# Attention with feed-forward on 8 cores: heads and output tiles transposed by DMA, and side work planned by its length

## The reference

```python
r = layernorm(x)                      # x: 4 x 4096 x 1024
q = einsum('bnd,hkd->bnhk', r, Wq)    # 16 heads of 64
k = einsum('bmd,dk->bmk', r, Wk)      # one key head, shared by all
v = einsum('bmd,dv->bmv', r, Wv)
o = softmax(q k^T / 8) v
x = x + einsum('bnhv,dhv->bnd', o, Wp)
s = layernorm(x) @ Win + bin          # 64 values per token
g = sum_h relu(s[..., None] * W1 + b1) * W2 + b2   # 16 inner values each
x = x + g @ Wout + bout
```

## Time and profile before

| | |
|---|---|
| time, median of 3 runs | 1017.74 us (1017.22 to 1017.86) |
| time of the profiled execution | 1017.6 us |
| its span on the slowest core | 1016.1 us (the 8 cores: 1012.9 to 1016.1) |
| busy: PE, PEld, DVE, ACT, POOL | 900.6, 493.1, 358.7, 952.2, 56.5 us |
| granted TensorE clock, mean of a core | 0.986 to 0.989 |
| chain that ended last | ACT 80%, issue 9%, PE 5%, DVE 3%, DMA 3% |

### The profile page before, as it was taken

One profiled execution on the slowest core, in us unless ns is written; L12 is line 12 of the kernel. 1 busy time (PEld: TensorE's weight loads), 2 busy tenths in 40 slices (PEclk: granted clock), 3 DMA queues, 4 the chain that ended last, 5 costly groups with the idle time before them and its releaser, 6 DMA issues.

```text
span 1016.1 us, 28595 instructions; the slowest of 8 cores (1012.9 to 1016.1 us)
## 1 busy us (share of the span) xinstructions
PE 900.6 (89%) x11582; PEld 493.1 (49%) x11712; DVE 358.7 (35%) x637; ACT 952.2 (94%) x1043; POOL 56.5 (6%) x131
## 2 busy tenths in 40 slices
PE   3898899998899999998889999998889998898884
PEld 3445555555444545544444454544444554454442
DVE  4535666652512222234202122244202326424215
ACT  2597999999999999999999999999999999999981
POOL 3201111100000000000000000000000000000000
PEclk9999999999999999999999999999999999999995
DMA  8502257220000000002200000001210000400101
GB/s 196 138 12 85 85 119 174 85 85 3 1 2 2 2 2 2 2 2 84 85 2 2 1 3 1 2 2 62 58 51 2 2 2 2 167 2 1 44 2 41
DMA packets 13406, 40.94 MB, mean 40 GB/s; under 512 B 3168, under 2 KB 3296, under 8 KB 13152
## 3 DMA queue, kind: packets, MB, share of 16 engines
q1 hardware_dynamic: 8208, 26.26, 8.5%
q0 software_dynamic: 4784, 12.32, 5.3%
q10 hardware_dynamic: 288, 0.52, 0.1%
HBM read 35.70 MB, written 8.39 MB: 43 GB/s over the span
## 4 chain that ended last, share of the span: by engine, by line
ACT 80%; issue 9%; PE 5%; DVE 3%; DMA 3%; POOL 0%; DVEq 0%; SPq 0%; POOLq 0%; ACTq 0%
ACT ptu L816 80%; DMA xtra<-x_own 2%; PE ob L457 1%; DMA xbuf<-x_own 1%; PE spa L662 1%; PE spb L662 1%; DVE r1u L478 1%; PE sda L380 0%; DVE r1t L504 0%; DVE lnst L468 0%; PE spb L695 0%; DVE lnst L469 0%; DVE gacc L787 0%; POOL rstd L838 0%; PE sdb L391 0%
## 5 line engine op out<-in xcount | busy, mean ns | idle before, releaser
L816 ACT ACTIVATE ptu<-spa 128x1024 bf16<-128x1024 f32 x512 | 594.5, 1161 | 17.7 <-PE spa L662 17.6
L816 ACT ACTIVATE ptu<-spb 128x1024 bf16<-128x1024 f32 x512 | 595.9, 1164 | 2.9 <-PE spb L662 2.9
L457 PE MATMUL ob<-vab,ptu 128*128 128x65 bf16 x8192 | 409.1, 195 | 0.7 <-ACT ptu L816 0.5
L457 PEld LDWEIGHTS ob<-vab,ptu 128*128 128x128 bf16 x8192 | 298.4, 97 | 208.4 <-issue 208.4
L662 PE MATMUL spb<-qt,k2t 64*128 64x512 bf16 x1024 | 200.8, 380 | 40.5 <-ACT ptu L816 34.9
L662 PE MATMUL spa<-qt,k2t 64*128 64x512 bf16 x1024 | 200.9, 380 | 36.5 <-ACT ptu L816 28.3
L662 PEld LDWEIGHTS spb<-qt,k2t 64*128 64x128 bf16 x1024 | 63.4, 92 | 127.2 <-issue 108.1
L662 PEld LDWEIGHTS spa<-qt,k2t 64*128 64x128 bf16 x1024 | 62.6, 92 | 114.5 <-issue 95.1
L725 DVE TENSOR_TENSOR oacc<-oacc,ob 128x520 f32<-128x520 f32 x50 | 34.8, 696 | 77.3 <-PE ob L457 77.2
L836 POOL TENSOR_SCALAR lnve<-lnmv 128x1 f32<-128x1 f32 x48 | 12.7, 264 | 658.0 <-DVE lnmv L471 658.0
L527 DVE TENSOR_TENSOR xbuf<-xbuf,sda 128x512 f32<-128x512 f32 x16 | 11.0, 688 | 93.3 <-PE sda L423 80.0
(11 more groups left out here) (123 smaller groups left out, 471.1 us busy)
## 6 DMA issues: line engine op xcount, KB each, us to landing
xbuf<-x_own SPq DMA_DIRECT2D x28, 512.0 KB, 4.4
xbuf<-x_oth SPq DMA_DIRECT2D x16, 512.0 KB, 3.9
out<-xbuf POOLq DMA_DIRECT2D x14, 512.0 KB, 3.6
wqb<-wq POOLq DMA_DIRECT2D x8, 256.0 KB, 9.6
xtra<-x_own SPq DMA_DIRECT2D x4, 512.0 KB, 6.9
xtra<-wp POOLq DMA_DIRECT2D x1, 2048.0 KB, 21.0
boutbc_s<-boutbc SPq DMA_DIRECT2D x1, 512.0 KB, 12.7
out<-xbuf SPq DMA_DIRECT2D x2, 256.0 KB, 2.6
```

Source lines behind the costliest of these rows:

```text
L457: r = te.matmul(osum[:, hd, c * 65:(c + 1) * 65], ptu[:, g % NPT, hd * 512 + c * 128:hd * 512 + (c + 1) * 128], vab[:, a + i, :], start=(i ...
L816: sc.activation(ptu[:, g % NPT, :], sps[g % 2][:], AF.Exp, scale=0.125).then_inc(ex, 1)
```

## The change

- The 31 "ot" transposes (all but the last pair of heads) and the 14 "rt" transposes leave PE and DVE. SP issues DMA transposes instead, from `on` to `ot` and from r1u to r2t, in an order (`moves`) that `pace` writes down; "op" and "s2" wait for their semaphores. In block 3 a pair of heads takes two DMAs.
- The loads of x for output tiles 4 to 15 move from SP to POOL, behind the stores of the tiles before them; wp is loaded in 8 DMAs instead of one.
- `pace` weighs pieces: a slot is 92 (hundredths of a us), scores 22, a half 12, a PE piece 22; a piece goes in while PE is at most 25 behind. DVE pieces have lengths of their own, and a tile's statistics are two pieces.
- What the value product needs is forced behind the scores, no longer ahead of them; V of slab 0 comes ahead of the first scores. K of slab 1 is made in two parts, three tiles and one. All queries of block 1 come at the end of block 0's list, those of block k + 1 in block k.
- r1u holds 4 tiles instead of 2.

```diff
-    o = [("V", 0, 0)] + q(0, 1) + slab(1) + [("V", 1, 0)]
-    o += q(0, 2, 3, 4, 5, 6, 7)
+    o = [("V", 0, 0)] + q(0, 1) + slab(1) + [("V", 1, 0)] + q(0, 2, 3, 4, 5, 6, 7)
     for s in range(2, NSLAB):
         o += slab(s) + [("V", s, 0)]
-    return o + q(1, 0) + [("ot", 0, hp) for hp in range(NHP - 1)]
+    return o + q(1, *range(NHP))
 def output_parts(b):
...
 def output_parts(b):
     op = [[("op", 4 * b + t, h) for h in range(2)] for t in range(4)]
-    rt = [("rt", 4 * b + t, 0) for t in range(4)]
     fo = [("fo", 4 * b + t, h) for t in range(4) for h in range(2)]
-    return [op[0], op[1], rt[0:1] + op[2], rt[1:2] + op[3], rt[2:4], [("s2", b, 0)], fo[0:4], fo[4:8]]
+    return op + [[], [("s2", b, 0)], fo[0:4], fo[4:8]]
...
-    queries = [("Q", 1, c) for c in range(1, NHP)] + [("Q", k, c) for k in (2, 3) for c in range(NHP)]
     o = []
     for p in range(24):
         k, i = 1 + p // NHP, p % NHP
         if i == 0:
-            o += [("ot", k - 1, NHP - 1)]
             parts = output_parts(k - 1)
-        for _ in range(1 + p % 2):
-            o += [queries.pop(0)] if queries else []
-        o += [("ot", k, i - 1)] if i else []
+        o += [("Q", k + 1, i)] if k < LAST else []
         if k < LAST:
             o += parts[i]
         elif i < 4:
             o += parts[2 * i] + parts[2 * i + 1]
         else:
             o += [[("op", 12, 0), ("op", 12, 1), ("op", 13, 0), ("op", 13, 1)],
...
+SLOT = 92
+SCORES = 22
+SWITCH = 20
+HALF = 12
+PIECE = 22
+PE_LAG = 25
+TR_LAG = 6
...
+    def force(want, where):
+        n = 0
+        while not ok(want, -TR_LAG):
+            mm = [("smd", v) for name, v in want if name == "sev"]
+            if not ok(mm, 0) and ok(head["pe"], -TR_LAG):
+                run("pe", pe, "pe" + where)
+                n += 1
+            else:
+                assert head["dve"] is not None and ok(head["dve"][0], -TR_LAG), (now, head)
+                run("dve", dve, "dve" + where)
+        return n
...
+            if g == -2:
+                want.append(("sev", USE_NO["V", 0, 0] + 1))
+            forced += force(want, "_s")
...
-        while not ok(want, 0):
-            if head["pe"] is not None and ok(head["pe"], 0):
-                run("pe", pe, "pe0")
-            else:
-                assert head["dve"] is not None and ok(head["dve"], 0), (g, head)
-                run("dve", dve, "dve0")
+                note("otd", 8 * SEGS[s][0] + SEGS[s][1] + 1, TR_LAG)
+            dve_lag += 110 if last_part(s) else 75
...
-        halves = len(pv_at(s, g - SEG_AT[s]))
-        for _ in range({0: 2, 2: 1, 3: 0}[halves]):
-            if head["pe"] is not None and ok(head["pe"], 1):
-                run("pe", pe, "pe1")
-
-        if g + 1 != SEG_AT[s + 1] and head["dve"] is not None and ok(head["dve"], 1):
-            run("dve", dve, "dve1")
-    return counts
+        halves = pv_at(s, g - SEG_AT[s])
+        forced += force([("sev", USE_NO["V", (SEGS[s][2] + h // 2) // 4, 0] + 1) for h in halves], "_v")
+        pe_lag = min(pe_lag + PIECE * forced, PE_LAG)
+        t = SCORES + HALF * len(halves) + (SWITCH if halves or forced else 0)
+        switch = 0 if halves or forced else SWITCH
+        while head["pe"] is not None and ok(head["pe"], 1):
+            if pe_lag + t + switch + PIECE - SLOT > PE_LAG:
+                break
+            run("pe", pe, "pe")
+            t += switch + PIECE
+            switch = 0
+        pe_lag = max(0, pe_lag + t - SLOT)
+        room = SLOT + (20 if g + 1 in SEG_AT else 115)
+        while head["dve"] is not None and ok(head["dve"][0], 1) and dve_lag + head["dve"][1] <= room:
+            dve_lag += head["dve"][1]
+            run("dve", dve, "dve")
+        dve_lag = max(0, dve_lag - SLOT)
+    return counts, moves
...
                 elif kind == "K":
-                    yield [("sev", n)]
-                    wait_ev(te, n - 1)
-                    for j in range(DCH):
-                        if j:
-                            yield []
-                        r = te.matmul(bank[:], wkb[:, j, :], r1t[:, slab_buf(a), j, :],
-                                      start=(j == 0), stop=(j == DCH - 1))
+                    parts = [(0, 3), (3, 4)] if a == 1 else [(0, 4)]
+                    for t0, t1 in parts:
+                        tr = USE_NO["tr", 4 * a + t1 - 1, 0]
+                        cols = slice(128 * t0, 128 * t1)
+                        for j in range(DCH):
+                            if j == 0:
+                                yield [free, ("sev", tr + 1)]
+                                wait_ev(te, n - 2)
+                                wait_ev(te, tr)
+                            elif j % (4 if t1 - t0 == 1 else 1) == 0:
+                                yield []
+                            r = te.matmul(bank[:, cols], wkb[:, j, :], r1t[:, slab_buf(a), j, cols],
+                                          start=(j == 0), stop=(j == DCH - 1))
...
-                    done = USE_NO["ot", blk, {0: NHP - 1, 12: 3, 14: 6}[a // 2 * 2 if blk == LAST else 0]]
-                    yield [free, ("sev", done + 1)]
+                    done = 8 * blk + ({12: 3, 14: 6}[a // 2 * 2] if blk == LAST else NHP - 1)
+                    yield [free, ("otd", done + 1)]
                     if a == 0 and b == 0:
-                        te.wait_ge(wpl, 16)
+                        te.wait_ge(wpl, 16 * DCH)
                     wait_ev(te, n - 2)
-                    wait_ev(te, done)
+                    te.wait_ge(otl[done % 2], heads_moved(done))
+                    te.wait_ge(otl[1 - done % 2], heads_moved(done - 1))
...
-                    yield [("sev", n)]
+                    li = NTILES + GROUPS[a][-1]
+                    yield [free, ("trd", li + 1)]
                     if a == 0:
                         te.wait_ge(winl, 16)
-                    wait_ev(te, n - 1)
+                    wait_ev(te, n - 2)
+                    for t in GROUPS[a]:
+                        te.wait_ge(trl[t % 4], 16 * (t // 4 + 1))
...
+            elif li < NTILES + 4:
+                if li >= 8:
+                    v.wait_ge(smd, USE_NO["tr", li - 4, 0] + 1)
+            else:
+                v.wait_ge(trl[q], 16 * ((li - NTILES) // 4))
+            v.tensor_scalar(r1u[:, q, :], xt(li), lnmv[:, q, 0:1], rstd[:, q, :],
                             op0=ALU.subtract, op1=ALU.mult).then_inc(nrm, 1)
...
-            te.wait_ge(pset, 1)
-            te.wait_ge(qev, 2)
             for g in range(-2, NG):
-                run(gen, counts["pe0"].get(g, 0))
+                run(gen, counts["pe_s"].get(g, 0))
+                if g == -2:
+                    te.wait_ge(pset, 1)
+                    te.wait_ge(qev, 2)
...
+                if i >= 24:
+                    c = i - 24
                     e.wait_ge(nrm, 8)
-                    e.dma_start(wpb, wp_d.rearrange("p (c d) -> p c d", d=D)).then_inc(wpl, 16)
+                    e.dma_start(wpb[:, c, :], wp_d[:, c * D:(c + 1) * D]).then_inc(wpl, 16)
             for ts in GROUPS[:-1]:
...
+                for t in ts:
+                    if t + 4 < OTILES:
+                        e.wait_ge(ost[t % 4], 16 * (t // 4 + 1))
+                        e.dma_start(xbuf[:, t % 4, :], xo_r[t + 4]).then_inc(xol[t % 4], 16)
...
+        def tile_transpose(e, li, dst):
+            e.wait_ge(nrm, li + 1)
+            e.dma_start_transpose(dst, r1u[:, li % 4, :]).then_inc(trl[li % 4], 16)
+        def head_transpose(e, k, i):
+            n = 8 * k + i
+            if i == 0 and k >= 2:
+                wait_ev(e, USE_NO["op", 4 * (k - 2) + 3, 1])
+            e.wait_ge(onr, n + 1)
+            if k < LAST:
+                e.dma_start_transpose(ot[:, k % 2, i, :].rearrange("p (c t) -> p c t", c=4),
+                                      on[:, n % 2].rearrange("p c t -> p (c t)")).then_inc(otl[n % 2], 16)
+            else:
+                q0 = 256 * (i // 4)
+                for c in range(2):
+                    e.dma_start_transpose(
+                        ot[:, k % 2, 2 * (i % 4) + c, q0:q0 + 256].rearrange("p (c t) -> p c t", c=2),
+                        on[:, n % 2, 2 * c:2 * c + 2].rearrange("p c t -> p (c t)")).then_inc(otl[n % 2], 16)
         @block.sync
         def _(e):
@@ -892,10 +983,15 @@
             for t in range(4):
                 e.wait_ge(nrm, NTILES - 3 + t)
                 e.dma_start(xbuf[:, t, :], xo_r[t]).then_inc(xl[t], 16)
...
-            for k in range(1, NK):
-                for t in range(4):
-                    e.wait_ge(ost[t], 16 * k)
-                    e.dma_start(xbuf[:, t, :], xo_r[4 * k + t]).then_inc(xl[t], 16)
+            for kind, n in moves:
+                if kind == "otd":
+                    if n < 8 * NK - 1:
+                        head_transpose(e, n // 8, n % 8)
+                    continue
+                t = n - NTILES
+                if t == GROUPS[GROUP_OF[t]][0]:
```

(2 more changed lines are left out.)

161 lines of the change are left out of this document (85 added, 76 removed).

## The result

The changed kernel took 1030.18 us (median of 4 runs, 1028.85 to 1031.06), the kernel before 1017.8 beside it: ratio 1.0122, 95% interval 1.0103 to 1.0142. It is slower by 12.4 us; the prediction said 1013.2, faster by 4.5, with a range that ended at 1018.5. Executions in which a whole die shows a lower granted clock are left out of the ratios here, but not out of the medians.

What follows compares the result with a forecast made beforehand. The prediction took ACT's 1,024 exponentials to bound the kernel, so only waits ahead of scores count. Its terms summed to -4.45 us, from 1017.6 to 1013.2, with a range for 8 in 10 of 1010 to 1018.5.

Steps and rivals of the forecast that it cites:

- Term 8: Denser packing of side work on PE, beside 12 value matmuls too: +1.2 us, bounds +0.5 and +3.
- The clock rival: PE's clock falls in slots 397 to 519 and 645 to 775, without side work: +60 us, 1075; chance 0.02.
- Term 7: Small waits for DVE's copies or o_out over the whole run, half of them gone: -1.5 us, bounds 0 and -2.5.
- Term 9: DMA transposes for "ot" and "rt" in place of PE and DVE work, landing in time: 0 us.
- The rival of late transposes: DMA transposes land late and block PE, then scores and ACT: slower, 1032.8 at a latency of 8 us; chance 0.14.
- Term 6: Slot 64, five K matmuls stay of the burst: loses 1.85 us where it lost 6.6, so -4.7 us.
- Term 5: Slot 24, a query ends right ahead of its first scores, without time for DVE's copy: a new stall, +1.0 us.
- Terms 1 and 2: V of slab 0 ahead of the first scores, slots 0 to 4: +0.2 us; K of slab 1 in parts, slot 8: -0.8.
- Terms 3 and 4: V of slab 1 behind scores 10, scores 12 queued behind: +0.4 us; fewer query matmuls ahead of slot 16: -0.25.

Runs made afterwards that it cites:

- e2: Changed kernel with at most one piece of side work beside 8 or 12 value matmuls, two beside none: 1027.61 us, ratio 1.0081 to the kernel before.
- e7: Changed kernel, side work gated by head pair, at most one piece beside 8 value matmuls, none beside 12 from slot 64, filler matmuls: 1020.78 us, ratio 1.0024.
- e1: Changed kernel with three unused 256-column matmuls in slots from 256 on without value product or side work: 1026.52 us, ratio 1.0066.
- e5: Changed kernel whose planner may start side work listed under a head pair only when that pair is done: 1025.59 us, ratio 1.0060.
- e3: Changed kernel with ordinary DMA copies of the same bytes in place of the DMA transposes: 1031.45 us, ratio 1.0111.
- b2: Kernel before with one piece also beside 12 value matmuls in slots 16 to 63, and K of slab 1 in two parts: 1012.40 us, ratio 0.9941.
- b4: b2 with V of slab 0 ahead of the first scores and DVE's copy of it ahead of following tiles' statistics: 1013.62 us, ratio 0.9953.

## Why the prediction was wrong

By its own steps:
- **Term 8, the packing, failed: it was priced for block 0 and one time only.** It said +1.2, at most +3, from a few slots a slab in four to five slabs, "less in the others". The new planner packs side work two deep or beside 12 matmuls in 152 slots behind slot 68. And "0.18 of it forgiven" is true once in 15 slots, since the reserve refills by 0.01 to 0.015 a slot. What packing costs behind slot 70 is the median core's time there without the falls of the clock: 886.7 us in the changed kernel, 881.3 in e2, 877.9 in e7, 877.7 before. So it is 9.0 where the term had 1.2, of which e2 takes the two-deep part (5.4, with the waits for DVE of 2.1 in it) and e7 the rest.
- **The clock rival had the right cause and the wrong place.** It asked of slots with value products and no side work (PE busy 16.31 of 20 us) whether the clock falls, found that it doesn't, which holds after too, and gave it 0.02. I did not ask it of the two slots without value products at a segment's start, PE busy 1.12 of 2. Each fall costs 0.8: 4.4 on the median core, 7.2 on the slowest, and none in e1. The Trainium skill, "TensorE: Matmul & The Clock Gate", Part 1, says that activity releases the clock; e1's windows agree (1.00 where they were 0.50 to 0.85).
- **Why those slots were bare** I had seen in the order and not read: I called the removed groups "worth 0 since these pieces stood in free room". Their matmuls were, but they held back the list behind them and filled these very slots. e5 shows both.
- **Term 7** (-1.5 for small waits that go) failed: they don't go, new ones come, the five for DVE (2.1 us on every core) among them. 878.55 in e7 and 878.05 before leave nothing for it.
- **Term 9** (0 for DMA transposes) was nearly right: e3's time can't be told from the changed kernel's, and e7 still has them. No transpose of the changed kernel took over 4.6 us, inside the 4.8 that the term allowed before "s2", and yet four cores waited 0.27 to 0.91 at slot 842: the term left out the 2.46 us in which SP issues two transposes of heads ahead of the tile's. The Trainium skill, "Advanced Engine Details and Errata", "X-Bar Transpose (TRN2)", has them as fast as ordinary DMAs; the landings of 3.1 and 2.9 us for 256 KB nearly agree. The rival of late transposes is real in e7, where they meet a load and take up to 7.2 us.
- **Term 6** (slot 64, -4.7) was right: the loss there is 1.91, worked out as 1.85. But it was sized on one core: the kernel before lost 6.4 there on its slowest core and 4.9 by the median of the eight, and on the median core slots 24 to 64 gain only 2.8 (39.31 for 42.12). **Term 5** (+1.0 at slot 24) was right: 1.0, and by the medians of the stretch from 16 to 24 1.1.
- **Terms 1 and 2**: K in parts gives 0.82 in b2, as said. V first was sized at +0.2 and costs about 0.7 (b4), so in the changed kernel slot 8 comes at the same time as before. **Terms 3 and 4** had +0.15 together for slots 8 to 16; the medians have +0.38 (9.88 for 9.50).

By the medians: +1.07 to the first exponential, -0.91 to slot 8, +0.38 to 16, +1.08 to 24, -2.81 to 64, -0.19 to 70, +13.99 behind it, together +12.6. Of the 13.99, 4.4 are falls of the clock, 5.8 small losses (7.3 for 1.5) and 2.1 the five waits for DVE. What stays open: the other 1.7, in single losses; why the clock falls at one bare start and not at the next; and the gaps of 0.6 to 1.7 in PE's own issue, which most kernels have on some cores between 153 and 250 us, the kernel before too. No run aims at them. The miss of 17 us is no bad luck: most of it is two costs, of packing and of bare starts, that the range left out and that could be counted in the new kernel's order.

## What to carry to other kernels

When work leaves an engine's list, ask of each removed piece what it held back and which thin slot it filled, not only what it cost; a planner that was steered by it will move everything else. A slack that is forgiven once is no price for a pattern that repeats: read how fast it refills. Read a price on all cores: the slowest one can be slow by that very loss (here nine falls of the clock for a median of 5.5). And before a rewrite of the planner, try the one number that holds the stall: here it gave 0.5%, and the rewrite cost 1.2%.

## What the hardware showed that I had not expected

- In a kernel whose PE is busy 87% of the time, the granted clock fell from 1.00 to 0.50 behind two slots with 0.39 us of matmuls in 0.92 each, at 3 to 9 of twelve such places on each core; the matmuls from 433.27 to some 437.0 show one fall, and these are the fullest slots. Slots with 8 value matmuls and no side work kept 1.00. Behind a wait of 1.79 us it fell as well (e7).
- DMA transposes between SBUF tiles took 2.4 us to landing for 64 and for 128 KB and 3.1 for 256 KB in the median, plain copies 1.9, 2.0 and 2.9. Beside a load, at 300 to 450 GB/s in all, two of 64 KB took 6.4 and 7.2. SP spends 1.19 us on issuing one of 128 KB (0.49 on a plain copy in e3):

```profile
402.78 1.19 SPq L955 DMA_TRANSPOSE ot<-on  x1
```
